# Masks of the shifted scores set by ScalarE, and three bank pairs divided anew

## The reference, cut to what matters

```python
attn = jnp.einsum('bhqd,bhkd->bhqk', q, k) * scale
block_mask = block_ids[:, None] != block_ids[None, :]
causal_mask = pos[:, None] < pos[None, :]
attn = jnp.where((causal_mask | block_mask)[None, None], mask_floor, attn)
attn = jax.nn.softmax(attn, axis=-1)
context = jnp.einsum('bhqk,bhkd->bhqd', attn, v)
```

## Time and profile before

| | us |
|---|---|
| median of 3 runs | 666.25 (665.54 to 667.37) |
| profiled execution | 665.03 |
| its span, first to last instruction | 663.2 |
| TensorE busy | 619.9 |
| VectorE busy | 404.6 |
| ScalarE busy | 315.7 |
| GpSimd busy | 185.2 |
| granted TensorE clock, mean | 0.978 of full speed |

### The profile page before, as it was taken

One profiled execution on the slowest core, in us unless ns is written; L12 is line 12 of the kernel. 1 busy time (PEld: TensorE's weight loads), 2 busy tenths in 40 slices (PEclk: granted clock), 3 DMA queues, 4 the chain that ended last, 5 costly groups with the idle time before them and its releaser, 6 DMA issues.

```text
span 663.2 us, 13983 instructions
## 1 busy us (share of the span) xinstructions
PE 619.9 (93%) x5816; PEld 424.9 (64%) x5816; DVE 404.6 (61%) x623; ACT 315.7 (48%) x478; POOL 185.2 (28%) x264
## 2 busy tenths in 40 slices
PE   5689999999999999999999999999999999869996
PEld 3545667567864667667884657766785566637783
DVE  2786744687467563668557555468647664447554
ACT  3736464356444356257443445437534444417442
POOL 1156640024016561034005662023102763000000
PEclk8599999999999999999999999999999999989999
DMA  8744000034022000025012100004202100000000
GB/s 327 239 111 119 30 3 1 1 83 109 1 60 99 2 2 3 0 48 144 1 27 70 64 3 2 1 14 123 57 0 64 65 2 3 1 1 0 1 1 32
DMA packets 16456, 31.77 MB, mean 48 GB/s; under 512 B 5060, under 2 KB 5828, under 8 KB 16260
## 3 DMA queue, kind: packets, MB, share of 16 engines
q1 hardware_dynamic: 14856, 27.98, 14.5%
q0 software_dynamic: 1152, 2.36, 1.4%
q10 hardware_dynamic: 384, 0.52, 0.3%
HBM read 12.99 MB, written 2.10 MB: 23 GB/s over the span
## 4 chain that ended last, share of the span: by engine, by line
PE 72%; DVE 14%; ACT 9%; issue 4%; DMA 1%; DVEq 0%; SPq 0%; ACTq 0%
PE bank L1622 8%; PE bank L1532 7%; PE bank L1424 5%; PE bank L1428 5%; PE bank L1425 5%; PE bank L1710 4%; PE bank L1560 3%; PE bank L1594 3%; PE bank L1805 3%; PE bank L1807 3%; PE bank L1568 3%; PE bank L1806 3%; PE bank L1831 2%; PE bank L1828 2%; PE bank L1464 2%
## 5 line engine op out<-in xcount | busy, mean ns | idle before, releaser
L1143 DVE TENSOR_REDUCE neg_max<-bank 128x8 f32<-128x1024 f32 x64 | 77.7, 1223 | 46.5 <-PE bank L1560 46.3
L584 POOL TENSOR_SCALAR arena_r<-q_st,const 100x512 fp32r<-100x512 f32 x128 | 87.7, 702 | 47.5 <-ACT q_st L778 47.1
L1332 DVE TENSOR_TENSOR arena<-arena,bank 128x512 f32<-128x512 f32 (+1 forms) x72 | 49.6, 688 | 71.7 <-ACT arena L870 69.9
L1424 PE MATMUL bank<-n_hi,w_lo 128*128 128x512 f32 x184 | 79.8, 434 | 3.3 <-ACT n_hi L733 1.7
L870 ACT ACTIVATE arena<-bank 128x512 f32<-128x512 f32 (+1 forms) x72 | 43.0, 598 | 82.0 <-PE bank L1807 47.0
L1532 PE MATMUL bank<-mask 128*128 128x512 bf16 x256 | 77.9, 386 | 3.6 <-ACT n_hi L683 2.2
L1428 PE MATMUL bank<-n_lo,w_hi 128*128 128x512 f32 x184 | 74.4, 404 | 0.2
L1425 PE MATMUL bank<-n_hi,w_hi 128*128 128x512 f32 x184 | 74.1, 403 | 0.0
L807 ACT ACTIVATE tile_f<-bank 128x1024 f32<-128x1024 f32 x56 | 57.2, 1024 | 33.4 <-PE bank L1594 33.2
L565 POOL TENSOR_TENSOR k_wide<-n_lo,head_of 128x512 fp32r<-128x512 f32 x30 | 32.6, 1089 | 103.9 <-DMA n_lo<-k_st 103.9
L539 POOL TENSOR_TENSOR tile_f<-tile_f,const 128x512 f32<-128x512 f32 x16 | 22.3, 1394 | 121.5 <-ACT tile_f L719 121.5
(11 more groups left out here) (180 smaller groups left out, 1167.9 us busy)
## 6 DMA issues: line engine op xcount, KB each, us to landing
q_st<-arena_r SPq DMA_DIRECT2D x96, 64.0 KB, 2.0
k_st<-arena_r SPq DMA_DIRECT2D x52, 64.0 KB, 2.0
k_st<-arena_r POOLq DMA_DIRECT2D x36, 64.0 KB, 2.4
h_next<-in_x SPq DMA_DIRECT2D x4, 512.0 KB, 3.6
tile_f<-in_x SPq DMA_DIRECT2D x4, 512.0 KB, 4.4
out<-arena SPq DMA_DIRECT2D x4, 512.0 KB, 2.8
n_lo<-k_st SPq DMA_DIRECT2D x24, 64.0 KB, 2.0
n_hi<-q_st SPq DMA_DIRECT2D x24, 64.0 KB, 2.0
```

Of the source, the lines that this page charges most:

```text
L584: last = nc.gpsimd.tensor_scalar(q_ex[u % 2][0:KS, :, hh, :], src, con("head")[0:KS, hh:hh + 1], 1.0, ALU.mult, ALU.mult)
L1143: nc.vector.tensor_reduce(neg_max[:, 2 * a:2 * a + 2, MROW:KS], slot(("s1", n)).rearrange("p a (h s) -> p a h s", s=P), AX_X, ALU.max, neg ...
L1332: nc.vector.tensor_tensor(pair_tmp[n % 2][0:width], silu_out[n % 2][0:width], up, ALU.mult)\
L1424: nc.tensor.matmul(to, wl[:, at], n_hi[:, kt, :], start=kt == 0, stop=False)
```

## The change

The list of pairs is divided anew: from the seventh fill on, S(even) has banks 0-1, S(odd) banks 4-5, and all M and T share banks 2-3. For units 1 to 6 (`PRESET`) ScalarE copies the mask into the pair of S one unit ahead: in unit u, after both exponentials, `preset` for 2(u+1) and 2(u+1)+1, each after the exponential that read that pair, ahead of the copy L814 and of the row cast. TensorE waits for `mask_set` instead of the pair and accumulates its scores on the copied values, without the two mask matmuls. These are 48 copies of 128 x 1024 in the whole kernel in place of 96 matmuls. Units 0 and 7 keep theirs. The order on TensorE in a unit becomes S(2u), M(2u+4), S(2u+1), C(2u), M(2u+5), C(2u+1), T(u+2).

```diff
--- before.py
+++ after.py
@@ -103,6 +103,7 @@
 CHUNK_WIDTHS += [SPLIT_COLS - sum(CHUNK_WIDTHS) - 2 * S, 2 * S]
 CHUNKS = [(sum(CHUNK_WIDTHS[:c]), width) for c, width in enumerate(CHUNK_WIDTHS)]
 LATE_CHUNK = 4
+PRESET = range(1, UNITS - 1)
 FIRST_CONST = CONST["ident"][0]
 
 
@@ -331,6 +332,7 @@
         lora_hi = signal("lora_hi", 4)
         powers_set = signal("powers_set", 1)
         exp_half = signal("exp_half", 2)
+        mask_set = signal("mask_set", 2 * len(PRESET))
         lora_lo = signal("lora_lo", 4)
         gu_ready = signal("gu_ready", FT * VARIANTS)
         ff_silu = signal("ff_silu", FT * VARIANTS)
@@ -353,8 +355,8 @@
                 fills += [("s2", 2 * u + a)] + ([("s1", 2 * (u + AHEAD) + a)] if u + AHEAD < UNITS else [])
             if u + AHEAD < UNITS:
                 fills += [("t", u + AHEAD)]
-        for n, what in enumerate(fills[6:]):
-            slot_of[what] = (n + 2) % 3
+        for kind, n in fills[6:]:
+            slot_of[kind, n] = 2 - n % 2 if kind == "s2" else 0
         freed_by = {"s1": max_done, "t": max_rows, "s2": exp_done}
 
         def slot(fill):
@@ -778,6 +780,12 @@
                 nc.scalar.copy(q_st[MROW:KS, half * GQ:(half + 1) * GQ, blk * P:(blk + 1) * P], src)\
                     .then_inc(max_rows.sem, 1)
 
+            def preset(row, n):
+
+                act.wait_ge(exp_done.sem, exp_done.count(row, n - 1))
+                to = slot(("s2", n)).rearrange("p g (h s) -> p (g h) s", s=P)
+                nc.scalar.copy(to, mask[:, 2:3, :].broadcast_to([P, 2 * GH, P])).then_inc(mask_set.sem, 1)
+
             def tails_stacked():
 
                 act.wait_ge(chunk_hi[5].sem, 1)
@@ -807,6 +815,8 @@
                             nc.scalar.activation(prob[a], scores, ACT.Exp, scale=SCALE).then_inc(exp_done.sem, 1)
                         if row == n == 0:
                             max_to_rows(0, 1, 0)
+                    for a in range(2) if u + 1 in PRESET else ():
+                        preset(row, 2 * (u + 1) + a)
                     if u == 0:
 
                         act.wait_ge(out_ready.sem, out_ready.count(row, 0))
@@ -1586,13 +1596,19 @@
                             half_stacked(pe, row, half, 0)
                         if u == BLOCKS:
                             pe.wait_ge(ones_back.sem, 16)
-                    to = fill(row, "s2", n, 0)
-                    for g in range(2):
-                        masked(to[:, g, :], 2)
+                    if u in PRESET:
+
+                        pe.wait_ge(mask_set.sem, mask_set.count(row, n - 2 * PRESET[0] + 1))
+                        to = slot(("s2", n))
+                    else:
+                        to = fill(row, "s2", n, 0)
+                        for g in range(2):
+                            masked(to[:, g, :], 2)
                     for g in range(2):
                         gq = 2 * a + g
                         last = nc.tensor.matmul(to[:, g, :], k_st[0:KS, half * GQ + gq, blk * P:(blk + 1) * P],
-                                                q_ex[u % 2][0:KS, gq], start=False, stop=True)
+                                                q_ex[u % 2][0:KS, gq], start=False, stop=True,
+                                                skip_group_check=u in PRESET)
                     last.then_inc(s2_ready.sem, 1)
 
                 def contexts(n):
@@ -1628,14 +1644,17 @@
                     shifted_scores(0)
                 max_transposed(row, 1, 0)
                 for u in range(UNITS):
-                    for a in range(2):
-                        if row or u or a:
-                            shifted_scores(2 * u + a)
-                        if u + AHEAD < UNITS:
-                            scores_for_max(row, 2 * (u + AHEAD) + a, 0)
-                    for a in range(2):
-                        contexts(2 * u + a)
-                    if u + AHEAD < UNITS:
+                    further = u + AHEAD < UNITS
+                    if row or u:
+                        shifted_scores(2 * u)
+                    if further:
+                        scores_for_max(row, 2 * (u + AHEAD), 0)
+                    shifted_scores(2 * u + 1)
+                    contexts(2 * u)
+                    if further:
+                        scores_for_max(row, 2 * (u + AHEAD) + 1, 0)
+                    contexts(2 * u + 1)
+                    if further:
                         max_transposed(row, u + AHEAD, 0)
                     if not is_last:
```

## The result

| | before | after |
|---|---|---|
| median of 4 runs, us | 666.81 (665.54 to 667.53) | 673.52 (672.46 to 674.29) |
| profiled execution / its span, us | 665.03 / 663.2 | 672.46 / 670.6 |
| a steady unit (row 3), T to T, us | 6.12 | 6.43 |
| attention of rows 0 to 3, first T to `o_proj`, us | 49.95, 49.20, 49.22, 45.48 | 52.06, 50.66, 50.60, 47.44 |

The kernel became 1.0% slower: ratio 1.0102, interval 1.0077 to 1.0126. Forecast were 0.6% and 670.2 us. The sign was right. 673.5 lies in the wider range that was stated (8 times in 10, 666.4 to 675.0), but outside the forecast's own, 667.7 to 672.5: the size is well short. Of the attention's +6.9 us in the two profiles the sum had 3.9. (Of the 3.3 us between 670.2 and 673.5, 0.6 is the base: with a fourth run the median of before is 666.81, where the sum had started from 666.25.)

The account below looks back on a forecast made before the run. TensorE, packed before, would wait on a loop through the shared pair, 6.30 us a unit for 6.12. Row 0 +1.3, rows 1 and 2 +1.4, last row +1.22: 3.9 us on 666.25 gives 670.2, range 667.7 to 672.5.

Parts of the forecast that it names:

- the masks' time turns into idle time: Steady unit: the 0.97 us of removed mask work becomes TensorE idle time, some 0.4 ahead of T and 0.3 ahead of M(even).
- The pieces of the loop: Steady unit through the shared pair: M(even), S(odd) 0.65, C(even) 1.01, M(odd), VectorE's 1.23, T, cast; 6.30 us for 6.12.
- The releases: Waits ahead of T and M(even): TensorE starts 0.04 or 0.05 us after VectorE, and 0.05 after the cast.
- "0.01" and "+0.24": Rows 1 and 2: unit 4, behind the squares, costs 0.01 us more; unit 5, where nothing waits for the cast, 0.24.
- the two delays: Row 0: its own casts on ScalarE behind the row cast make two delays of about 0.3 us, row total +1.3.
- Unit 0: First unit, masks kept: M(even) of unit 1 begins at 7.72 us instead of 7.01, a cost of 0.71.
- the queue on ScalarE behind the copy L814: Unit 0: exponential, two copies and L814 hold the row cast until 7.09 us; 0.18 of the unit's 0.71.
- The copy: ScalarE's mask copy into a bank: 1.02 us, bounds 0.9 and 1.5, hidden in a steady unit.
- the rival with the dear copy: ScalarE: at 1.5 us a copy the cast waits; unit 0 loses 0.96 more, others 0.1; 676 us. Chance 0.12.
- The end of a row: Units 6 and 7, without M and led by ScalarE: first exponential comes one mask pair earlier, -0.45 us.
- A unit as short as before: Rival: S without load 0.57 and C(even) 0.94 give a loop of 6.15 us; total 666.6 us. Chance 0.20.
- TensorE leads throughout: Rival: the pair comes free before TensorE wants it; units of 5.4 us, -16 us in four rows, 650 us. Chance 0.06.

## Why the prediction was right or wrong

**That the masks' time turns into idle time: right.** TensorE idles ahead of T behind VectorE's reduction, and ahead of M(even) behind the cast, in each of units 0 to 4, 0.40 and 0.29 long for the forecast 0.4 and 0.3 (by the forecast's own sum, 5.93 to 6.30, the second is 0.37). TensorE's total fell by 8.9, a little under the 10 to 20 that were named, and in the unit with the mean the idle time ahead of M(even) is gone (7.33 busy of 7.73, the 0.40 ahead of T is left); it is 0.10 shorter (0.18 forecast).

**The pieces of the loop: right.** M(even) took 1.02 (forecast 0.97), S(odd) 0.65 (0.65), C(even) 1.01 (1.01), M(odd) to its reader 1.00 for 1.09, the maximum 1.24 (1.23), T to the cast 0.65 for 0.68.

**The releases: the step that failed.** The waits and their order were right; the term of the loop's sum that was mis-sized is how long TensorE takes to begin once its wait is over. "T starts 0.04 or 0.05 after VectorE" and "With 0.05 for the release the next M(even) begins at 6.30": 0.04 and 0.05 in the sum, 0.14 and 0.14 measured. I took them from a T of unit 0, whose second wait, through `fill`, is for the first of its two maxima and had been served a microsecond before; in units 2 to 7 both waits are for the last one. The listing of the kernel had the two waits ahead of T and of M(even) in plain view, and I read them only for what they wait for. 6.30 + 0.10 + 0.09, less 0.05 for the small pieces together (M(odd) and T under the sum, M(even) at 1.02 for 0.97 over it), is 6.44; the stretch is 6.43. The run with the waits rewritten gets 6.30 and returns 2.07 of the missing 3.0 us.

**The other 0.9 us** remain in that run: 0.46 in row 0, 0.24 and 0.22 in rows 1 and 2, 0.01 in row 3. What rows 1 and 2 have and row 3 lacks is the work for a next row. In after's row 1 the two units behind the squares grew by 0.67 and -0.02, 0.65 together, where "0.01" and "+0.24" stood in the sum. Between the masks of M(even), the first of the two took 7.44 us, for 7.14: 0.09 of it is the release ahead of T, 0.03 the exponential, and 0.18 T and S(even) on both sides of the sums of squares, 0.54 and 0.58 for 0.48 and 0.46. These two I had taken from the packed neighbours and not from beside a 32-column operation. In the 0.03 hides another long wake: the exponential ended 0.06 earlier than forecast, and TensorE began C(even) 0.14 behind it, with 0.05 in the sum. The run with the waits rewritten left this one as it is. Row 0 has two more of them, where its casts of late weights delay the exponential: in that run its units 1 and 2 grew by 0.61 each (T to T, 6.38 to 6.99 and 6.98 to 7.59) and row 1's by 0.19 and 0.18. That is 0.42 for each of the two delays, where the forecast had about 0.3, and with the 0.24 of row 1 it makes the 0.46 of row 0. In the old order it was a mask of M that waited there, and in row 0 of before it began at 66.05, 0.05 behind the exponential's end.

**Unit 0: right in its sum, wrong in a part.** From its first mask to M(even) of unit 1 it took 7.70 us (forecast 7.72). But "only then the cast, 7.67", the queue on ScalarE behind the copy L814 (L824 in after), was not what held it. ScalarE in unit 0 of row 1 (start, duration, work, idle ahead and who ended it):

```profile
210.55 1.96 ACT L787 CAST bank<-mask 128x1024 f32<-128x1024 bf16 x2
212.43 1.05 ACT L824 COPY h<-h_next 128x1024 f32<-128x1024 f32 x1
213.63 0.58 ACT L780 CAST q_st<-bank 4x512 fp32r<-4x512 f32 x1 [0.15 <-PE bank L1578]
```

The cast waited for T. The two copies and L824 start 0.94 after one another, so L824 ended 6.82 into the unit, not at 7.09, and the cast began at 6.97. T, at 6.32, had come 0.09 late, and the wake behind the cast was 0.15: the two long releases filled what the queue gave up, and the total agreed by accident.

**The copy: right.** 1018 ns for the forecast 1.02, so the rival with the dear copy fell by its own number. The run with a further copy shows what a dear one would have cost: about 0.9 in unit 0, as written, 0.7 to 0.9 at row 0's casts, which the rival did not name, and nothing in a steady unit, where it had 0.1. The Trainium skill (ScalarE: Activation LUTs, on what happens in an exp ACTIVATE) says that ScalarE writes banks faster than the other memory. The trace agrees in sign, at 3%: 1018 ns here, 1.05 us for the copy L824 of as many values. The two differ in the type that they read too (bf16 and fp32), so the runs do not show that the target is the reason.

**The end of a row:** -0.45 forecast for units 6 and 7, -0.45 in row 1 (9.82 to 9.37), -0.33 in row 3.

**The rivals.** A unit as short as before fell: S(odd) and C(even) were at my middle values, not at their lower bounds, and even with the short releases the unit stays at 6.30. The switches cost what the rows said; the Trainium skill's rule (TensorEngine Tiling (Array Packing), Key Properties) that a change of mode drains the array agrees with the 0.54 of a mask pair behind contexts and with S at 0.67 there (0.43 and 0.47 without a switch). That TensorE leads throughout fell too: the loop of two maxima, cast and T is over 6 us, as argued against it. Units below 6.0 came only when T had left that loop.

**My reading of the change** was still too narrow in one point: I saw the new order as what makes C(even) cover the first maximum, and not what it takes from the second. The order alone costs 0.60 a unit (6.72 for 6.12), the division alone 0.55 (6.67), and both together 0.67, so the two do not add up.

## What to carry to other kernels

Work taken from the busiest engine is worth only the distance to the next closed loop: before removing it, write that loop down (who reads what, who refills it) and see whether the change makes it longer by putting more users on one buffer. Price a wake by the number of waits that stand ahead of the instruction: if one of them is implied by another drop it, and write the one that comes last in time first, so that the load of weights carries it. If two users share a buffer and one of them holds it for a hand-over between engines, move that one to a buffer that is idle at the time. Here the other bank alone turned 1.0% slower into 0.6% slower; with T a step later, the squares moved and the even exponential in halves it became 0.7% faster.

## What the runs showed of the hardware

- TensorE's wake after another engine's end took 0.04 to 0.05 us in one writing of the waits and 0.14 in another, with the same work on both sides. It showed behind VectorE, behind ScalarE's cast and behind its exponential.
- TensorE's granted clock stayed at 1.00 (2.4 GHz) through the idle times of 0.3 to 0.4 in every unit of after's rows 1 to 3. In the run with a further copy it stood at 0.50 (1.2 GHz) some two microseconds after one idle time of 1.21, with 32 matmuls at 1.87 for 1.01 us, but stayed at 1.00 after the same idle time in the three other rows. In nine of the eleven profiles the last matmuls ran at 0.50 too (1061 for 592 ns); before's and that of the run with T at its old place did not.
- ScalarE writes a mask from memory into a pair of banks (bf16 to fp32, 1024 columns) in 1018 ns, and two of them in 1.96 us.
- A pair of scores for 100 rows cost 0.46 to 0.47 behind masks, 0.65 directly behind scores of 32 rows, and 0.67 behind contexts of 32 columns: about 0.2 us, as much as one load of its weights (0.19), which in the trace starts only with the scores there and runs beside the masks else.
